# Layer norm moved from GpSimd to VectorE, and one more slot in two weight rings, in a transformer block on eight cores

## The chip, the cores and the metric

The kernel runs on the 8 cores of one Trainium2 chip, one program on every core, with no exchange between them. Cores 0 to 3 work on the first batch element and cores 4 to 7 on the second. The metric is the device time in microseconds of the slowest core.

## The reference

The block adds an attention branch and a feed-forward branch, both fed by the same layer norm, to the input `x` of shape (2, 4096, 2048):

```python
xn = layernorm(x)                                    # over 2048 features
q, k = rope(xn @ Wq.T), rope(xn @ Wk.T)              # 16 heads, each two halves of 64
v = xn @ Wv.T                                        # 16 heads of 128
o1, o2 = softmax(q1 k1 / 8) v, softmax(q2 k2 / 8) v
attn = rmsnorm(o1 - lam * o2) * gamma * (1 - LAMBDA_INIT)
ffn = ((silu(xn @ Wg.T * gs)) * (xn @ Wu.T * us)) @ Wd.T * ds    # 5632 inner features
out = x + attn @ Wo.T + ffn
```

## The kernel before, in words

The program that runs is `build_F` (`build_A` and `build_B` are an older pair that is not launched). A core owns 1024 tokens of the output, but computes K and V for all 4096 tokens of its batch element itself. Activations lie transposed: features on the 128 partitions, tokens along the free dimension, so a tile of x is 128 features by 512 tokens.

**K and V.** The 4096 tokens are taken in four chunks of 1024; chunk 0 holds the core's own tokens. For each chunk come the layer norm (`emit_ln`), the K projection (16 output chunks `och`, each 32 matmuls, L1065, then rope on VectorE and a maximum of squares) and the V projection (`emit_vproj_cache`, eight groups of 64 matmuls, L1455, emptied by ScalarE). In chunk 0 the fp32 weights are cast by their loads and also stored as bf16 copies (`wk_c`, `wv_c`) that the other chunks read.

**Layer norm.** `emit_ln` works on two tiles of 512 tokens. In each it reads x twice, in four quarters of 4 k-chunks (1 MB each), through a ring `rx` of two slots on SyncE's queue (L172):

- The statistics pass: per k-chunk, GpSimd casts x to bf16 (L186), ScalarE squares it (L188), and TensorE sums both over the partitions with a column of ones (L192, L195).
- A short chain on one partition makes mean and 1/sqrt(var + eps) (L200 to L208), and TensorE spreads both over the 128 partitions into PSUM `ps_b` (L212, L214). ScalarE copies them to SBUF as `mB_sb` and `rB_sb` (L217, L218), since GpSimd's operands lie in SBUF.
- The normalise pass: for each of 16 k-chunks GpSimd subtracts the mean (L227) and multiplies by rstd (L229) into the bf16 operand of the projections.

**Feed-forward.** After the Q projection, for each of two tiles of 512 tokens: 44 chunks of gate and up (32 matmuls, L1156 and L1161 in turn, then ScalarE's Silu and two VectorE instructions that end in `h_bf`), and then 16 chunks `hch` of the down projection, each two halves of 22 matmuls (L1200 with the first half of the weights, L1207 with the second). The weights come through rings in one SBUF tensor `wffn`, loaded by GpSimd's DMA queue: `gring` (2 slots, L1147), `uring` (2 slots, L1149) and `dring` (3 slots, L1190 and L1192; a chunk takes two slots).

Then follow attention over all 4096 keys for 16 heads, and the output projection.

**What sets the order.** There is no scheduler. `Prog` keeps one list of instructions for each engine in the order in which the Python code emits them, and each engine runs its list in that order, its waits and the DMAs that it issues included. Each instruction with a count also waits for the one before it on its own engine (except on TensorE). A ring's load waits until the work that `consumed` noted for its slot is done:

```python
        slot = i % n
        if i >= n:
            for sem, val in self.done[i - n].items():
                self.p.wait(self.queue, sem, val)
```

`gring.consumed`, `uring.consumed` and `dring.consumed` note the count of TensorE at the end of the whole chunk, for both of its loads. The first matmul of the K projection waits for the value that `emit_ln` returns (all of the layer norm's arithmetic) and for its `wbuf` load (L1050 in chunk 0, L1057 later), which GpSimd issues.

Of the kernel before, what the change touches and what calls it, by code (L numbers as in the profile page):

```python
# [8 lines left out]
F32 = mybir.dt.float32  # L9
# [116 lines left out]
def alloc_common(nc, ent, t):  # L126
# [18 lines left out]
    t["eps_col"] = ent(nc.sbuf_tensor("eps_col", [128, 1], F32))  # L145
    t["mB_sb"] = ent(nc.sbuf_tensor("mB_sb", [128, 512], F32))
    t["rB_sb"] = ent(nc.sbuf_tensor("rB_sb", [128, 512], F32))
    t["plt"] = ent(nc.sbuf_tensor("plt", [128, 512], F32))
    t["trow"] = ent(nc.sbuf_tensor("trow", [1, 16], F32))
# [14 lines left out]
def emit_ln(p, t, x_hbm, xn_bf, xn_seg, xn_col0, ring=None):  # L164
# [12 lines left out]
    for tile in range(2):  # L177
        p.wait("pe", "dv", t.get("hn_dv", 0))
        for q in range(4):
            i, sl, key = qload(q, tile)  # L180
            p.wait("pool", *key)
            p.wait("act", *key)
            for j in range(4):
                kch = q * 4 + j
                co = sl * 2048 + j * 512
                p.inc("pool", "pl", 1, lambda E, co=co: E.tensor_copy(  # L186
                    xbb[:, co:co + 512], xc[:, co:co + 512]))
                p.inc("act", "ac", 1, lambda E, co=co: E.activation(  # L188
                    x2b[:, co:co + 512], xc[:, co:co + 512], AF.Square))
                p.wait("pe", "pl")  # L190
                p.wait("pe", "ac")
                p.emit("pe", lambda E, co=co, kch=kch: E.matmul(  # L192
                    ps_d1[:], t["ones_col_bf"][:], xbb[:, co:co + 512],
                    start=(kch == 0), stop=(kch == KCH - 1)))
                mmv = p.inc("pe", "pe", 1, lambda E, co=co, kch=kch: E.matmul(  # L195
                    ps_d2[:], t["ones_col_bf"][:], x2b[:, co:co + 512],
                    start=(kch == 0), stop=(kch == KCH - 1)))
            ring.consumed(i, "pl", "ac", "pe")
        p.wait("act", "pe", mmv)
# [10 lines left out]
        p.wait("pe", "dv")  # L210
        p.wait("pe", "pl")
        p.emit("pe", lambda E: E.matmul(ps_b[:, 0:512], t["ones_row_f"][:], row[0:1, 0:512],  # L212
                                        start=True, stop=True))
        bcv = p.inc("pe", "pe", 1, lambda E: E.matmul(  # L214
            ps_b[:, 512:1024], t["ones_row_f"][:], row[0:1, 1536:2048], start=True, stop=True))
        p.wait("act", "pe", bcv)
        p.inc("act", "ac", 1, lambda E: E.activation(t["mB_sb"][:], ps_b[:, 0:512], AF.Copy))  # L217
        brv2 = p.inc("act", "ac", 1, lambda E: E.activation(t["rB_sb"][:], ps_b[:, 512:1024], AF.Copy))  # L218
        for q in range(4):
            i, sl, key = qload(q, tile)  # L220
            p.wait("pool", *key)
            p.wait("pool", "ac", brv2)
            for j in range(4):
                kch = q * 4 + j
                co = sl * 2048 + j * 512
                c0 = xn_col0 + tile * 512
                p.inc("pool", "pl", 1, lambda E, co=co: E.tensor_tensor(  # L227
                    t["plt"][:, 0:512], xc[:, co:co + 512], t["mB_sb"][:], ALU.subtract))
                p.inc("pool", "pl", 1, lambda E, kch=kch, c0=c0: E.tensor_tensor(  # L229
                    xn_bf[:, kch * xn_seg + c0: kch * xn_seg + c0 + 512],  # L230
                    t["plt"][:, 0:512], t["rB_sb"][:], ALU.mult))
            ring.consumed(i, "pl")
    return {"pl": p.ct["pl"]}

# [195 lines left out]
def build_B(debug=False):  # L430
# [30 lines left out]
    t = {}  # L461
# [14 lines left out]
    t["eps_col"] = ent(nc.sbuf_tensor("eps_col", [128, 1], F32))  # L476
    t["mB_sb"] = ent(nc.sbuf_tensor("mB_sb", [128, 512], F32))
    t["rB_sb"] = ent(nc.sbuf_tensor("rB_sb", [128, 512], F32))
    t["plt"] = ent(nc.sbuf_tensor("plt", [128, 512], F32))
    t["bias_sb"] = ent(nc.sbuf_tensor("bias_sb", [128, 16], F32))  # L480
# [414 lines left out]
def build_F(debug=False):  # L895
# [48 lines left out]
    t["eps_col"] = ent(nc.sbuf_tensor("eps_col", [128, 1], F32))  # L944
    t["mB_sb"] = ent(nc.sbuf_tensor("mB_sb", [128, 512], F32))
    t["rB_sb"] = ent(nc.sbuf_tensor("rB_sb", [128, 512], F32))
    t["plt"] = ent(nc.sbuf_tensor("plt", [128, 512], F32))
    t["bias_sb"] = ent(nc.sbuf_tensor("bias_sb", [128, 16], F32))
# [185 lines left out]
    t["h_bf"] = ent2(nc.sbuf_tensor("h_bf", [128, ICH * 512], BF16, side="right"))  # L1134
    t["wffn"] = ent2(nc.sbuf_tensor("wffn", [128, 8448], BF16, side="right"))
    gring = Ring(p, "rg", 2, "pool")
    uring = Ring(p, "ru", 2, "pool")
    dring = Ring(p, "rd", 3, "pool")
    wffn = t["wffn"]
    UOFF = 4096  # L1140
    for tile in range(2):
# [454 lines left out]
```

How the kernel before makes its waits and increments, by code:

```python
    def wait(self, eng, sem, val=None):  # L41
        v = self.ct[sem] if val is None else val
        if v <= 0:
            return
        s = self.sems[sem]
        self.emit(eng, lambda E, s=s, v=v: E.wait_ge(s, v))
# [3 lines left out]
    def inc(self, eng, sem, n, mk):  # L50
        own = self.OWN.get(eng)
        if own is not None and self.ct[own] > 0:
            self.wait(eng, own)
        if n >= 16 and sem == "lds" and self.ct[sem] > 0:
            self.wait(eng, sem)
        s = self.sems[sem]
        self.ct[sem] += n
        v = self.ct[sem]
        self.emit(eng, lambda E, mk=mk, s=s, n=n: mk(E).then_inc(s, n))
        return v
```

## Time and profile before

| What | us |
|---|---|
| Two timed executions | 6734.73 and 6789.26 |
| Their median | 6761.99 |
| The profiled execution, its own time | 6545.5 |
| Its span, slowest core (core 5) | 6544.0 |
| Shortest core's span (core 4) | 6505.0 |
| TensorE busy in the span | 4297.3 |
| ScalarE busy | 1742.8 |
| VectorE busy | 846.9 |
| GpSimd busy | 608.1 |

The span runs from the first to the last instruction of one core. In the trace PE is TensorE, DVE VectorE, ACT ScalarE, POOL GpSimd and SPq or POOLq the DMA queues of SyncE and GpSimd. A row of a group gives its busy time, the mean of one instruction, and the time that its engine stood idle just before it, with what ended that wait. "PEclk" is the granted TensorE clock as a share of 2.4 GHz; 0.5 is the 1.2 GHz level. Matmul lengths overlap: at the full level one starts 0.216 us after the other though each row shows 0.38.

### The profile page before, as it was taken

The numbers are of one execution on the slowest core, as the hardware profiler recorded it, in microseconds if no ns is written. First come the engines' busy times: TensorE is split into PE (matmuls) and PEld (weight loads), VectorE is DVE, ScalarE is ACT, GpSimd is POOL, SyncE is SP. The second block draws the span as 40 slices with busy tenths as digits, with TensorE's granted clock in tenths as the row PEclk, the third lists the DMA queues.
The fourth block names the chain that finished last, engine by engine and source line by source line (L and its number), as shares of the span: only waits on it lengthen the run. The fifth ranks groups of instructions, "written<-read, shape, count | busy, mean of one in ns | idle before, by whom it ended". The sixth has DMA issues, their size and how long they took to land.

```text
span 6544.0 us, 47810 instructions; the slowest of 8 cores (6505.0 to 6544.0 us)
## 1 busy us (share of the span) xinstructions
PE 4297.3 (66%) x16260; PEld 1362.7 (21%) x16260; DVE 846.9 (13%) x1492; ACT 1742.8 (27%) x1879; POOL 608.1 (9%) x786
## 2 busy tenths in 40 slices
PE   2457255725653566557777777777777878787877
PEld 0113012201221122122233332311111111111113
DVE  0230033003201321321100111000000000000002
ACT  1011110111111111100000000046666666666650
POOL 5100600050024000000100000000000000000000
PEclk6679577856786788679988999888888888888889
DMA  3234311321132122135555555511000100000005
GB/s 112 73 85 152 112 39 58 138 83 40 74 124 77 39 82 84 26 58 97 97 96 97 101 98 93 106 39 26 13 13 13 26 13 13 23 17 13 13 10 145
DMA packets 177301, 428.87 MB, mean 66 GB/s; under 512 B 75944, under 2 KB 75944, under 8 KB 170152
## 3 DMA queue, kind: packets, MB, share of 16 engines
q0 software_dynamic: 55872, 272.65, 19.1%
q1 hardware_dynamic: 121192, 153.16, 7.6%
q8 instruction: 136, 2.23, 0.1%
q14 instruction: 101, 0.83, 0.0%
HBM read 539.02 MB, written 58.72 MB: 91 GB/s over the span
## 4 chain that ended last, share of the span: by engine, by line
PE 61%; DVE 11%; ACT 9%; DMA 8%; issue 6%; POOL 5%; DVEq 0%; ACTq 0%; SPq 0%; POOLq 0%
PE ps_a L1065 9%; PE ps_a L1455 7%; PE ps_b L1292 6%; PE ps_a L1156 5%; PE ps_a L1266 5%; PE ps_a L1161 5%; PE ps_d L1302 5%; PE ps_b L1297 4%; PE ps_d L1306 3%; DMA wffn<-dn 3%; PE ps_b L1207 3%; POOL plt L227 2%; PE ps_a L297 2%; POOL xnb L229 2%; DMA xc<-xTb 2%
## 5 line engine op out<-in xcount | busy, mean ns | idle before, releaser
L1286 ACT ACTIVATE e<-ps_a,bias_sb 128x1024 bf16<-128x1024 f32 x1024 | 1140.3, 1114 | 455.5 <-PE ps_a L1271 452.5
L1156 PE MATMUL ps_a<-xn_bf,wffn 128*128 128x512 bf16 x1408 | 572.8, 407 | 277.7 <-DVE h_bf L1182 259.6
L1161 PE MATMUL ps_a<-xn_bf,wffn 128*128 128x512 bf16 x1408 | 571.5, 406 | 0.0
L260 PE MATMUL ps_d<-sq_b,mask_bf 128*1 128x512 bf16 x160 | 93.6, 585 | 707.0 <-ACT sq_b L255 523.0
L1065 PE MATMUL ps_a<-xnb,wbuf 128*128 128x512 bf16 x1536 | 432.9, 452 | 154.3 <-DMA wbuf<-wk_c 154.3
L1266 PE MATMUL ps_a<-q_bf,ktb 64*128 64x512 bf16 x1024 | 416.2, 413 | 111.2 <-DVE xn_bf L1351 98.8
L1292 PE MATMUL ps_b<-e,vtb 128*128 128x512 bf16 x1024 | 405.2, 396 | 56.2 <-ACT e L1286 42.3
L239 ACT ACTIVATE qraw_bf<-ps_a 128x1024 bf16<-128x1024 f32 x80 | 81.9, 1023 | 1286.7 <-PE ps_a L1065 1057.9
L1271 PE MATMUL ps_a<-q_bf,ktb 64*128 64x512 bf16 x1024 | 417.2, 414 | 0.0
L1297 PE MATMUL ps_b<-e,vtb 128*128 128x512 bf16 x1024 | 406.1, 397 | 0.0
L1306 PE MATMUL ps_d<-e,ones_col_bf 128*1 128x512 bf16 x1024 | 402.4, 393 | 0.0
L1455 PE MATMUL ps_a<-wvbuf,xnb 128*128 128x512 bf16 x1536 | 358.5, 397 | 64.8 <-ACT v_stage L1467 64.8
L1302 PE MATMUL ps_d<-e,ones_col_bf 128*1 128x512 bf16 x1024 | 399.7, 390 | 0.0
L1174 ACT ACTIVATE tmp<-ps_a,gs_sb 128x512 f32<-128x512 f32 x88 | 60.5, 687 | 1116.4 <-PE ps_a L1161 1116.4
L192 PE MATMUL ps_d<-xbb,ones_col_bf 128*1 128x512 bf16 x128 | 70.0, 547 | 296.0 <-POOL xbb L186 293.4
L1065 PEld LDWEIGHTS ps_a<-xnb,wbuf 128*128 128x128 bf16 x1536 | 169.7, 113 | 437.3 <-issue 321.4
L1207 PE MATMUL ps_b<-h_bf,wffn 128*128 128x512 bf16 x704 | 201.4, 454 | 84.5 <-DMA wffn<-dn 84.5
L1329 DVE TENSOR_SCALAR r2B<-r2B,lam_vec 128x512 f32<-128x512 f32 x32 | 15.6, 486 | 1846.8 <-ACT r2B L1327 1846.8
L1156 PEld LDWEIGHTS ps_a<-xn_bf,wffn 128*128 128x128 bf16 x1408 | 145.7, 103 | 499.4 <-issue 362.2
L1376 POOL DMA_DIRECT2D wbuf<-wo x16 | 8.4, 528 | 2233.9 <-issue 2099.6
L1467 ACT ACTIVATE v_stage<-ps_a 128x512 bf16<-128x512 f32 x128 | 76.4, 597 | 516.2 <-PE ps_a L1455 507.5
L1266 PEld LDWEIGHTS ps_a<-q_bf,ktb 64*128 64x128 bf16 x1024 | 93.5, 93 | 572.9 <-issue 572.9
(123 smaller groups left out, 4038.3 us busy)
## 6 DMA issues: line engine op xcount, KB each, us to landing
wffn<-gu POOLq DMA_DIRECT2D x176, 512.0 KB, 7.0
xc<-xTb SPq DMA_DIRECT2D x64, 1024.0 KB, 5.3
wvbuf<-wv_c POOLq DMA_DIRECT2D x28, 2048.0 KB, 8.7
wffn<-dn POOLq DMA_DIRECT2D x64, 704.0 KB, 8.4
wbuf<-wk_c POOLq DMA_DIRECT2D x48, 512.0 KB, 3.5
kT_s<-kstage SPq DMA_DIRECT2D x64, 256.0 KB, 2.4
v_s<-v_stage SPq DMA_DIRECT2D x32, 512.0 KB, 5.5
ktb<-kT_s SPq DMA_DIRECT2D x16, 1024.0 KB, 5.1
```

Source lines behind the costliest of these rows:

```text
L1065: mm = lambda E, och=och, kch=kch, half=half, par=par, slot=slot, xn_dst=xn_dst: E.matmul(t["ps_a"][:, par * 1024 + half * 512: par * 1024 ...
L1156: p.emit("pe", lambda E, kch=kch, par=par, tile=tile, gsl=gsl: E.matmul(t["ps_a"][:, par * 1024: par * 1024 + 512], wffn[:, gsl * 2048 + k ...
L1161: mm = lambda E, kch=kch, par=par, tile=tile, usl=usl: E.matmul(t["ps_a"][:, par * 1024 + 512: par * 1024 + 1024], wffn[:, UOFF + usl * 20 ...
L1207: mm = lambda E, ich=ich, par=par, s1=s1: E.matmul(t["ps_b"][:, par * 512:(par + 1) * 512], wffn[:, s1 * 2816 + (ich - 22) * 128: s1 * 281 ...
L1266: p.emit("pe", lambda E, b=b, par=par, koff=koff, qcol=qcol: E.matmul(ps_a[:, par * 1024: par * 1024 + 512], t["ktb"][0:64, koff + b * 128 ...
L1271: return p.inc("pe", "pe", 1, lambda E, b=b, par=par, koff=koff, qcol=qcol: E.matmul(ps_a[:, par * 1024 + 512: par * 1024 + 1024], t["ktb" ...
L1286: ev = p.inc("act", "ac", 1, lambda E, par=par, h=h: E.activation(t["e12"][:, par * 1024:(par + 1) * 1024], ps_a[:, par * 1024:(par + 1) * ...
L1292: p.emit("pe", lambda E, b=b, par=par, koff=koff, first=first, last=last: E.matmul(ps_b[:, 0:512], t["vtb"][:, koff + b * 128: koff + (b + ...
L1297: p.emit("pe", lambda E, b=b, par=par, koff=koff, first=first, last=last: E.matmul(ps_b[:, 512:1024], t["vtb"][:, koff + b * 128: koff + ( ...
L1302: p.emit("pe", lambda E, par=par, first=first, last=last: E.matmul(ps_d1[:], t["ones_col_bf"][:], t["e12"][:, par * 1024: par * 1024 + 512 ...
L1306: mmD = lambda E, par=par, first=first, last=last: E.matmul(ps_d2[:], t["ones_col_bf"][:], t["e12"][:, par * 1024 + 512: par * 1024 + 1024 ...
L1455: mm = lambda E, kch=kch, tc=tc, tok=tok, slot=slot: E.matmul(vps(tc), xn_bf[:, kch * xn_seg + tok: kch * xn_seg + tok + 128], t["wvbuf"][ ...
```

## The change

The layer norm's arithmetic leaves GpSimd. VectorE casts x in the statistics pass, and in the normalise pass it reads mean and rstd straight from `ps_b` in PSUM, with `tmp0` as the intermediate. The copies `mB_sb`, `rB_sb` and the tensors `mB_sb`, `rB_sb` and `plt` go (6 KB a partition). The waits on GpSimd's count `pl` become waits on VectorE's count `dv`, and two waits of TensorE go: one on `dv` at the start of a tile (the values that it covered are waited for again later) and one on `pl` ahead of the broadcast. `wffn` grows from 8448 to 11264 columns, `gring` gets a third slot and `dring` a fourth; `uring` keeps two.

```diff
@@ emit_ln, statistics pass @@
-        p.wait("pe", "dv", t.get("hn_dv", 0))
         for q in range(4):
             i, sl, key = qload(q, tile)
-            p.wait("pool", *key)
+            p.wait("dve", *key)
             p.wait("act", *key)
...
-                p.inc("pool", "pl", 1, lambda E, co=co: E.tensor_copy(
+                p.inc("dve", "dv", 1, lambda E, co=co: E.tensor_copy(
                     xbb[:, co:co + 512], xc[:, co:co + 512]))
...
-                p.wait("pe", "pl")
+                p.wait("pe", "dv")
                 p.wait("pe", "ac")
...
-            ring.consumed(i, "pl", "ac", "pe")
+            ring.consumed(i, "dv", "ac", "pe")
@@ emit_ln, broadcast and normalise pass @@
-        p.wait("pe", "pl")
...
-        p.wait("act", "pe", bcv)
-        p.inc("act", "ac", 1, lambda E: E.activation(t["mB_sb"][:], ps_b[:, 0:512], AF.Copy))
-        brv2 = p.inc("act", "ac", 1, lambda E: E.activation(t["rB_sb"][:], ps_b[:, 512:1024], AF.Copy))
         for q in range(4):
             i, sl, key = qload(q, tile)
-            p.wait("pool", *key)
-            p.wait("pool", "ac", brv2)
+            p.wait("dve", *key)
+            p.wait("dve", "pe", bcv)
...
-                p.inc("pool", "pl", 1, lambda E, co=co: E.tensor_tensor(
-                    t["plt"][:, 0:512], xc[:, co:co + 512], t["mB_sb"][:], ALU.subtract))
-                p.inc("pool", "pl", 1, lambda E, kch=kch, c0=c0: E.tensor_tensor(
+                p.inc("dve", "dv", 1, lambda E, co=co: E.tensor_tensor(
+                    t["tmp0"][:, 0:512], xc[:, co:co + 512], ps_b[:, 0:512], ALU.subtract))
+                p.inc("dve", "dv", 1, lambda E, kch=kch, c0=c0: E.tensor_tensor(
                     xn_bf[:, kch * xn_seg + c0: kch * xn_seg + c0 + 512],
-                    t["plt"][:, 0:512], t["rB_sb"][:], ALU.mult))
-            ring.consumed(i, "pl")
-    return {"pl": p.ct["pl"]}
+                    t["tmp0"][:, 0:512], ps_b[:, 512:1024], ALU.mult))
+            ring.consumed(i, "dv")
+    return {"dv": p.ct["dv"]}
@@ build_F, feed-forward @@
-    t["wffn"] = ent2(nc.sbuf_tensor("wffn", [128, 8448], BF16, side="right"))
-    gring = Ring(p, "rg", 2, "pool")
+    t["wffn"] = ent2(nc.sbuf_tensor("wffn", [128, 11264], BF16, side="right"))
+    gring = Ring(p, "rg", 3, "pool")
     uring = Ring(p, "ru", 2, "pool")
-    dring = Ring(p, "rd", 3, "pool")
+    dring = Ring(p, "rd", 4, "pool")
     wffn = t["wffn"]
-    UOFF = 4096
+    UOFF = 6144
```

Three places of the program show what moves. The first is VectorE's list at the start of chunk 0. Before the change, two one-row subtracts (one for each tile of 512 tokens) stand between the copy of lambda and the rope work of the K projection:

```order
L993 COPY lam_vec<-ps_b 128x1
L204 TENSOR_TENSOR row<-row 1x512 x2
L241 STREAM_SHUFFLE tswp_bf<-qraw_bf 128x1024
L242 TENSOR_TENSOR tmpa_bf<-qraw_bf,ctab 128x1024
L244 TENSOR_TENSOR tswp_bf<-tswp_bf,stab 128x1024
```

With the change (its line numbers are lower) the same place begins so, with 15 more pairs of subtract and multiply behind the last row before the second tile's casts:

```order
L979 COPY lam_vec<-ps_b 128x1
L182 CAST xbb<-xc 128x512 x16
L200 TENSOR_TENSOR row<-row 1x512
L219 TENSOR_TENSOR tmp<-xc,ps_b 128x512
L221 TENSOR_TENSOR xn_bf<-tmp,ps_b 128x512
```

The 16 casts and 32 arithmetic instructions of each tile now stand in VectorE's list ahead of the rope work of the same chunk.

The second place is GpSimd's list from the V projection of chunk 0 to the K projection of chunk 1. Before, the loads of `wv_c` are followed by the casts and the arithmetic of chunk 1's two tiles, and only then come the `wk_c` loads; this is the second tile's start:

```order
L227 TENSOR_TENSOR plt<-xc,mB_sb 128x512
L229 TENSOR_TENSOR xnb<-plt,rB_sb 128x512
L186 CAST xbb<-xc 128x512 x16
L227 TENSOR_TENSOR plt<-xc,mB_sb 128x512
L229 TENSOR_TENSOR xnb<-plt,rB_sb 128x512
```

With the change there is nothing between the two kinds of loads:

```order
L1428 DMA wv_c<-wvbuf 128x8192
L1432 DMA wvbuf<-wv_c 128x8192 x4
L1043 DMA wbuf<-wk_c 128x2048 x16
L1432 DMA wvbuf<-wv_c 128x8192 x8
L1043 DMA wbuf<-wk_c 128x2048 x16
```

The `wk_c` loads have moved up past 96 instructions of the layer norm on that queue.

The third place is GpSimd's list where the down projection starts, with the semaphores that each row waits for (`pe` is TensorE's count, `pl` GpSimd's own). Before:

```order
L1190 DMA wffn<-dn 128x2816 [waits pe,pl]
L1192 DMA wffn<-dn 128x2816 [waits pl]
L1190 DMA wffn<-dn 128x2816 [waits pl]
L1192 DMA wffn<-dn 128x2816 [waits pe,pl]
L1190 DMA wffn<-dn 128x2816 [waits pe,pl]
```

And with the change:

```order
L1176 DMA wffn<-dn 128x2816 [waits pe,pl]
L1178 DMA wffn<-dn 128x2816 [waits pl]
L1176 DMA wffn<-dn 128x2816 [waits pl]
L1178 DMA wffn<-dn 128x2816 [waits pl]
L1176 DMA wffn<-dn 128x2816 [waits pe,pl]
```

The order of the loads is the same; the second half of the second chunk no longer waits for TensorE to finish the first chunk, and so on for each later second half, which waits for the chunk before last in place of the last.

## Rows read from the trace of the kernel before

**Rows 1.** Stages: length, busy time by engine (count), granted clock, DMA share, GB/s.

```profile
650.00:812.00 162.00, 31.85 (x73) 7.52 (x74) 1.36 (x2) 28.83 (x46) 101.44 (x98) 0.57 0.37 122
1128.00:1277.00 149.00, 121.70 (x513) 51.84 (x512) 1.65 (x4) 19.11 (x32) 3.17 (x6) 0.92 0.28 104
3348.00:3582.00 234.00, 179.65 (x704) 73.85 (x704) 13.33 (x18) 0.00 (x0) 18.54 (x36) 0.86 0.55 100
```

**Rows 2.** Page, the chain that ended last: shares of the span by line.

```profile
PE ps_a L1065 9%; PE ps_a L1455 7%; PE ps_b L1292 6%; PE ps_a L1156 5%; PE ps_a L1266 5%; PE ps_a L1161 5%; PE ps_d L1302 5%; PE ps_b L1297 4%; PE ps_d L1306 3%; DMA wffn<-dn 3%; PE ps_b L1207 3%; POOL plt L227 2%; PE ps_a L297 2%; POOL xnb L229 2%; DMA xc<-xTb 2%
```

**Rows 3.** Groups by line: forms, count | busy us, mean ns | idle before.

```profile
L227 POOL TENSOR_TENSOR plt<-xc,mB_sb 128x512 f32<-128x512 f32 x128 | 161.4, 1261 | 109.4 <-ACT rB_sb L218 92.2
L186 POOL CAST xbb<-xc 128x512 bf16<-128x512 f32 x128 | 78.5, 613 | 238.9 <-DMA xc<-xTb 224.6 <-POOL xbb L186 0.4
L188 ACT ACTIVATE x2b<-xc 128x512 bf16<-128x512 f32 x128 | 80.6, 629 | 291.2 <-DMA xc<-xTb 281.6 <-ACT x2b L188 0.4
```

**Rows 4.** Timeline of chunk 1, first tile: start, length us, engine, line.

```profile
684.81 1.91 PE L214 MATMUL ps_b<-row,ones_row_f 1*128 1x512 f32 x2
688.37 1.26 POOL L227 TENSOR_TENSOR plt<-xc,mB_sb 128x512 f32<-128x512 f32 x1 [11.17 <-ACT rB_sb L218]
...
733.30 2.85 POOL L186 CAST xbb<-xc 128x512 bf16<-128x512 f32 x4
```

**Rows 5.** Groups by line on VectorE, attention stage.

```profile
L1331 DVE TENSOR_TENSOR tmp<-ps_b,r1B 128x512 f32<-128x512 f32 x32 | 22.1, 691 | 3.3
L1349 DVE TENSOR_TENSOR tmp<-tmp,rstdB 128x512 f32<-128x512 f32 x32 | 22.1, 692 | 104.3 <-ACT rstdB L1346 104.3
L1329 DVE TENSOR_SCALAR r2B<-r2B,lam_vec 128x512 f32<-128x512 f32 x32 | 15.6, 486 | 1846.8 <-ACT r2B L1327 1846.8
```

**Rows 6.** Timeline of VectorE in one attention tile.

```profile
5002.94 0.69 DVE L1331 TENSOR_TENSOR tmp<-ps_b,r1B 128x512 f32<-128x512 f32 x1
5003.74 0.69 DVE L1333 TENSOR_TENSOR tmp<-ps_b,r2B 128x512 f32<-128x512 f32 x1
```

**Rows 7.** Landing of x loads (L172): whole span, then 690 to 735 us.

```profile
DMA to landing us min/median/max: 5.0/5.3/14.4
...
DMA to landing us min/median/max: 5.1/5.1/5.1
```

**Rows 8.** Timeline of chunk 0, then the chain of chunk 1: into the K projection.

```profile
182.02 1.26 POOL L229 TENSOR_TENSOR xn_bf<-plt,rB_sb 128x512 bf16<-128x512 f32 x1
190.39 1.86 PE L1065 MATMUL ps_a<-xn_bf,wbuf 128*128 128x512 bf16 x4 [53.55 <-DMA wbuf<-wk]
...
806.33 1.27 POOL xnb L229
...
811.94 8.75 PE ps_a L1065 x32
```

**Rows 9.** Down matmuls: two groups by line, then the line L1207 (min/median/max).

```profile
L1207 PE MATMUL ps_b<-h_bf,wffn 128*128 128x512 bf16 x704 | 201.4, 454 | 84.5 <-DMA wffn<-dn 84.5
L1200 PE MATMUL ps_b<-h_bf,wffn 128*128 128x512 bf16 x704 | 160.4, 385 | 16.6 <-DMA wffn<-dn 16.6
...
L1207 PE MATMUL ps_b<-h_bf,wffn x704: 376/379/634, 3361.3 to 4282.5; 128*128 128x512 bf16 x176
```

**Rows 10.** Timeline of the first down stretch.

```profile
3366.78 0.53 POOL L1192 DMA_DIRECT2D wffn<-dn  x1 [17.16 <-PE ps_b L1207]
3374.26 6.59 PE L1207 MATMUL ps_b<-h_bf,wffn 128*128 128x512 bf16 x22 [3.34 <-DMA wffn<-dn]
...
3486.47 4.91 PE L1207 MATMUL ps_b<-h_bf,wffn 128*128 128x512 bf16 x22 [2.13 <-DMA wffn<-dn]
```

**Rows 11.** Landing of the `dn` loads: first halves (L1190), then second halves (L1192).

```profile
DMA to landing us min/median/max: 7.2/9.1/14.0
...
DMA to landing us min/median/max: 5.9/6.3/10.9
```

**Rows 12.** The group of gate matmuls.

```profile
L1156 PE MATMUL ps_a<-xn_bf,wffn 128*128 128x512 bf16 x1408 | 572.8, 407 | 277.7 <-DVE h_bf L1182 259.6 <-DMA wffn<-gu 18.1
```

More of the change, by code:

```diff
@@ L145, in alloc_common @@
     t["eps_col"] = ent(nc.sbuf_tensor("eps_col", [128, 1], F32))
-    t["mB_sb"] = ent(nc.sbuf_tensor("mB_sb", [128, 512], F32))
-    t["rB_sb"] = ent(nc.sbuf_tensor("rB_sb", [128, 512], F32))
-    t["plt"] = ent(nc.sbuf_tensor("plt", [128, 512], F32))
     t["trow"] = ent(nc.sbuf_tensor("trow", [1, 16], F32))
@@ L476, in build_B @@
     t["eps_col"] = ent(nc.sbuf_tensor("eps_col", [128, 1], F32))
-    t["mB_sb"] = ent(nc.sbuf_tensor("mB_sb", [128, 512], F32))
-    t["rB_sb"] = ent(nc.sbuf_tensor("rB_sb", [128, 512], F32))
-    t["plt"] = ent(nc.sbuf_tensor("plt", [128, 512], F32))
     t["bias_sb"] = ent(nc.sbuf_tensor("bias_sb", [128, 16], F32))
@@ L944, in build_F @@
     t["eps_col"] = ent(nc.sbuf_tensor("eps_col", [128, 1], F32))
-    t["mB_sb"] = ent(nc.sbuf_tensor("mB_sb", [128, 512], F32))
-    t["rB_sb"] = ent(nc.sbuf_tensor("rB_sb", [128, 512], F32))
-    t["plt"] = ent(nc.sbuf_tensor("plt", [128, 512], F32))
     t["bias_sb"] = ent(nc.sbuf_tensor("bias_sb", [128, 16], F32))
@@ L1134, in build_F @@
     t["h_bf"] = ent2(nc.sbuf_tensor("h_bf", [128, ICH * 512], BF16, side="right"))
-    t["wffn"] = ent2(nc.sbuf_tensor("wffn", [128, 8448], BF16, side="right"))
-    gring = Ring(p, "rg", 2, "pool")
+    t["wffn"] = ent2(nc.sbuf_tensor("wffn", [128, 11264], BF16, side="right"))
+    gring = Ring(p, "rg", 3, "pool")
     uring = Ring(p, "ru", 2, "pool")
-    dring = Ring(p, "rd", 3, "pool")
+    dring = Ring(p, "rd", 4, "pool")
     wffn = t["wffn"]
-    UOFF = 4096
+    UOFF = 6144
     for tile in range(2):
```

## The prediction

> **What bounds the kernel now.** I read the stage table first [rows 1]. In the layer-norm stretch 650 to 812 us TensorE is busy 32 of 162 us and GpSimd 101; in the down stretch 3348 to 3582 us TensorE is busy 180 of 234 us, at a granted clock of 0.86. The kernel has eight such layer-norm tiles (two per chunk) and two down stretches. The shares of the chain that ended last [rows 2] name what stands there: GpSimd's L227 and L229 and the loads of `dn` and of x are on it, beside the long TensorE stages that the change leaves alone. The table of groups gives the durations [rows 3], and the timeline of one tile the order [rows 4]: the broadcast matmul L214 ends at 686.72, GpSimd's first subtract starts at 688.37, after ScalarE's two copies, and GpSimd works without a gap until 733.30, when it casts the first quarter of the next tile. So the normalise pass is GpSimd's alone, 44.9 us a tile, and the statistics pass is paced by ScalarE, which takes 629 ns beside a cast of 613 ns, and by the loads of x that both wait for.
>
> **The change part by part.**
>
> *Normalise pass.* One k-chunk costs GpSimd a subtract (L227, 1261 ns) and a multiply (L229), with 1.404 us from start to start (32 of them in 44.93 us). VectorE is to do the same two. Its multiply with one fp32 operand in PSUM takes 691 ns, and one with both in SBUF 692 ns [rows 5]; two dependent ones start 0.80 us apart [rows 6]. So 32 x 0.797 = 25.5 us in place of 44.9: 19.4 us a tile, 155.5 us over eight. Both ends for the instruction not seen in this exact pairing: 486 ns (L1329, the quickest VectorE pass over 512 fp32 elements here [rows 5]) gives another 50 us, 1261 ns (GpSimd's own) gives nothing; I take 691, a row of nearly the same form. The Trainium skill (VectorE: DVE Perf Modes, The TRN2 errata) states a fixed cost of 120 cycles for a VectorE operation with a PSUM source against 58 from SBUF. By that table 256 instructions would give back about 17 us, an estimate from its 0.96 GHz. The two rows of 691 and 692 ns show no such difference, and the measurement decides.
>
> *Does the load keep up?* Each quarter of x (1 MB) will be eaten in 6.4 us in place of 11.2. In the normalise pass a quarter landed 5.1 us after its issue [rows 7], and with two slots it has the 6.4 us of its neighbour: 1.3 us to spare. That cover is thin, and a rival below rests on it. The next tile's first quarters keep their distance to the end of this pass, so its statistics pass is as long as before.
>
> *ScalarE's two copies* go. GpSimd started 1.65 us after the matmul's end; VectorE needs about 0.15 for the hop: 1.5 us a tile, 12 us. *The casts* move to VectorE. Its one-input pass takes 486 ns and its slowest row of this size 692; by the first the cast lies within ScalarE's 629 ns, by the second 0.06 us x 128 = 8 us stick out. It has one input in SBUF like L1329, so I take 486 and a cost of nothing; if ScalarE were quicker, the cast would set the pace with 0.6 us. In VectorE's queue the casts stand behind the previous chunk's K work, finished a whole V stretch (149 us) before, and the tile-end subtract L204 stands behind normalise work that it waited for anyway through the statistics.
>
> *GpSimd's queue is empty of arithmetic.* So the first two `wbuf` loads of a chunk, which stood behind 96 GpSimd instructions of the layer norm, are issued in the V stretch before, where they have the whole layer-norm stretch of 162 us to land. The last GpSimd instruction ended at 183.28 and the K projection started at 190.39; in chunk 1 it was 807.60 and 811.94 [rows 8]. That is 7.1 and 4.3 us, and I take 4.3 for the other two: 20 us, less 0.3 us each for the semaphore: 19 us. Bounds 0 (something else is late too) and 20.
>
> *Down projection.* TensorE waited 84.5 us for the second half of `dn` (L1207), 30 times, and two starts of a stage for the first half (L1200) [rows 9]. With three slots the second half of chunk h+1 may be issued only when chunk h has ended; in the timeline it is issued at 3366.78 and TensorE waits until 3374.26 [rows 10]. With four it is issued a whole chunk earlier. The 84.5 us go, the two starts stay. What is late next? A chunk's matmuls at the 2.4 GHz level are 44 x 4.75 / 22 = 9.5 us (L1207 started at 3486.47 and lasted 4.91 with the last drain, about 4.75 to the next start). The transfers of a chunk, both issued 0.55 us apart, land after 6.3 and 9.1 us at the median [rows 11], so a pair needs 9.65 us and has until the chunk after next. The two are nearly level.
>
> *The clock in the down stage.* After the wait the 22 matmuls took 6.59 us, and elsewhere 4.91 [rows 10]. L1207 has a mean of 454 ns against a median of 379 and a maximum of 634 [rows 9]: (454 - 379) / (634 - 379) = 29% of 704, or 207 matmuls, ran at the 1.2 GHz level; L1200, mean 385, adds 17. At half rate each starts 0.21 us later: 224 x 0.21 = 47 us. The Trainium skill (TensorE: Matmul & The Clock Gate, Part 1) says that the throttled state is the default and activity lifts it. By that rule all 47 come back; by the row alone none need, since some gaps of 2 us, as before 3486.47, cost no clock at all. The V stretch, almost without gaps, shows 0.92 [rows 1]. I take 40, bounds 0 and 47. Down: 84.5 + 40 = 125 us, bounds 60 (transfers stretched, below) and 131.
>
> *The gate ring's third slot.* TensorE waits there for VectorE's `h_bf`, 259.6 us of L1156's idle time, and for a load only 18.1 us at two starts [rows 12]. The `gate` load is issued one chunk earlier, the `up` load not, and TensorE needs both: nothing. On GpSimd's queue the `up` load now goes ahead of the next `gate` load when a chunk ends, where it stood behind one, so it isn't slowed. Bounds: 18 us lost (the starts take twice as long) and 18 won.
>
> *Sum.* 155.5 + 12 + 19 + 125 = 311 us. The profiled execution took 6545.5 us (span 6544.0, so 1.5 us lie around it) and would take 6234. The two runs shown, 6734.7 and 6789.3, are 3% longer than it, with a median of 6762; I take the same 311 us off that: **6451 us**, 4.6% less.
>
> **The rivals.**
>
> *B, transfers bound the down stage.* A chunk reads 2 x 128 x 2816 x 4 bytes = 2.88 MB. To do that every 9.5 us in place of 14 ((234 - 10) / 16 [rows 1]), all eight cores draw half as much again. For it: L1190's slowest landing is 14.0 us [rows 11]. Against it: the DMA engines are busy 0.55 of that stretch [rows 1], and 0.55 x 14 = 7.7 us of their time fit into 9.5. If a pair takes 12.5 us, the gain is 32 x (14.0 - 12.5) = 48, and with little of the clock back some 60 in all: 6451 + 65 = 6516.
>
> *C, the x loads bound the normalise pass.* It begins once a quarter lands later than 6.4 us. For it: the slowest of the 64 x loads took 14.4 us. Against it: the median of all is 5.3, and all four in one normalise pass took 5.1 [rows 7]. At 8 us a quarter the pass takes 32 us: 8 x 6.5 = 52 us less gain, 6503.
>
> *D, slower: VectorE's PSUM operand.* Place: the 256 instructions that read the broadcast mean and rstd from `ps_b` while x comes from SBUF as fp32. If each took 2.6 us start to start, a tile would take 83 us, 38 more than now: 8 x 38 = 306 us lost against 156 from the other terms: 6762 + 306 - 156 = 6912. It decides from 2.0 us on, where a tile loses the 19.5 us that the others bring. Against it: 691 ns [rows 5].
>
> *E, the fourth slot does nothing*, because issue order on GpSimd or the landing itself holds the halves: the 125 us fall away, 6762 - 186 = 6576.
>
> *F, within 2%:* C and E together leave 311 - 52 - 125 = 134 us, 6628.
>
> **How the numbers follow.** Forecast 0.61, B 0.18, C 0.09, E 0.05, F 0.05, D 0.02. A measurement of this kernel can tell about 2% from no change, 135 us. Forecast, B, C and E lie beyond it: faster 0.93; F gives same 0.05; D slower 0.02. The forecast's own spread is 280 to 330 us. To that comes the spread of the executions of before, 6545.5 to 6789.3: taken from the shortest, the best case is 6545 - 325 = 6220; the upper end takes in B: 6530.
>
> **What would show it.** Right: VectorE's subtract and multiply at 0.69 us, 25 to 26 us a tile; the K projection's first matmul under 0.5 us after the last of them; no wait for `dn` at the second half but at most the first chunk, and a mean near 390 ns for those matmuls; a layer-norm stretch of about 116 us in place of 162; gate and up, K, V and attention stretches as before. Wrong: waits of VectorE for `xc` within the normalise pass (C); waits for `dn` at every chunk (B); a VectorE mean above 0.8 us (D); a lower granted clock in the stages the change leaves alone, which no term here contains.

## Result and profile after

The changed kernel took 6484.3 us (median of 12 executions, 6223.8 to 6646.1), the kernel before 6721.9 us (median of 10, 6558.5 to 6867.0). The ratio is 0.9488 with a 95% interval of 0.9448 to 0.9529. The prediction was 6451 us in a range of 6220 to 6530.

Executions of one kernel differ by up to 7%, and in the long ones the four cores of one die, or of both, show a lower granted clock; what follows therefore compares dies (by the median span of their four cores) that lie within 0.5% of the shortest of their kernel. Their median is 6527 us for the kernel before (32 dies) and 6217 us for the changed one (18 dies): 310 us or 4.7% less, where 311 us were forecast. The ratio above, from the slowest core of each execution, says 5.1%. In the profiled execution the slowest core is core 3 with 6261.2 us; its granted clock is 0.816, and that of core 5, which is read below because the rows of before are core 5's too, is 0.820 at a span of 6224.3 us.

The stage table of the changed kernel, core 5 (stretch, length, busy time by engine with count, granted clock, DMA share, GB/s), answers to [rows 1]. The stretches are one chunk's layer norm, its V projection, a first gate and up stretch and a down stretch:

```profile
601.00:720.00 119.00, 33.60 (x74) 8.53 (x75) 59.00 (x98) 26.45 (x42) 0.00 (x0) 0.56 0.48 151
1037.00:1178.00 141.00, 113.54 (x513) 49.99 (x512) 1.66 (x4) 19.11 (x32) 4.22 (x8) 0.98 0.32 118
2675.00:3162.00 487.00, 343.12 (x1410) 142.43 (x1411) 63.48 (x88) 31.53 (x45) 47.79 (x91) 0.91 0.55 97
3162.00:3322.00 160.00, 154.79 (x704) 69.09 (x702) 12.01 (x16) 0.00 (x0) 17.43 (x33) 0.98 0.80 140
```

Chunk 1's layer norm takes 118.7 us from the issue of its first load of x to the first K matmul (600.86 to 719.52) where it took 159.3 (652.66 to 811.94). The first down stretch takes 156.2 us from its first matmul to the end of its last (3161.60 to 3317.82) where it took 223.2 (3354.83 to 3578.01), at a granted clock of 0.98 in place of 0.86 and with the DMA engines busy 0.80 of the time in place of 0.55. GpSimd is idle in the layer norm and VectorE busy for 59 us. Over the whole core the time went like this:

| Part (core 5) | before us | after us | difference | forecast |
|---|---|---|---|---|
| four layer norms, first load of x to first K matmul | 652.9 | 470.2 | -182.7 | -186.5 |
| feed-forward, first load to the first attention matmul | 1432.7 | 1297.4 | -135.3 | -125 |
| all else | 4458.4 | 4456.7 | -1.7 | 0 |
| span | 6544.0 | 6224.3 | -319.7 | -311 |

The groups by line of the layer norm, core 5 (form, count | busy us, mean ns | idle just before and its releasers), answer to [rows 3]:

```profile
L219 DVE TENSOR_TENSOR tmp<-xc,ps_b 128x512 f32<-128x512 f32 x128 | 88.0, 687 | 60.5 <-PE ps_b L209 46.1 <-DMA xc<-xTb 1.3 <-DVE xn_bf L221 0.5
L221 DVE TENSOR_TENSOR xnb<-tmp,ps_b 128x512 bf16<-128x512 f32 x96 | 66.0, 687 | 10.0
L182 DVE CAST xbb<-xc 128x512 bf16<-128x512 f32 x128 | 54.6, 427 | 547.0 <-DMA xc<-xTb 535.9 <-DVE xbb L182 1.0
L184 ACT ACTIVATE x2b<-xc 128x512 bf16<-128x512 f32 x128 | 80.6, 630 | 236.8 <-DMA xc<-xTb 227.4
```

Subtract and multiply cost 687 ns, with 0.80 us from one to the next in the rows below (139.79, 140.59). The cast costs 427 ns, well inside ScalarE's 630. In the normalise pass VectorE waited for x for 1.3 us in all ("DMA xc<-xTb 1.3"), so the loads kept up with the faster pass. The timeline of core 5 at the end of chunk 0's and of chunk 1's layer norm answers to [rows 8]:

```profile
139.79 0.69 DVE L219 TENSOR_TENSOR tmp<-xc,ps_b 128x512 f32<-128x512 f32 x1
140.59 0.69 DVE L221 TENSOR_TENSOR xn_bf<-tmp,ps_b 128x512 bf16<-128x512 f32 x1
141.53 1.87 PE L1051 MATMUL ps_a<-xn_bf,wbuf 128*128 128x512 bf16 x4 [26.03 <-DVE xn_bf L221]
...
718.59 0.69 DVE L221 TENSOR_TENSOR xnb<-tmp,ps_b 128x512 bf16<-128x512 f32 x1
719.52 2.72 PE L1051 MATMUL ps_a<-xnb,wbuf 128*128 128x512 bf16 x6 [26.42 <-DVE xnb L221]
```

The K projection starts 0.25 us after the last multiply ends (140.59 + 0.69 = 141.28 to 141.53; 719.28 to 719.52), where it had started 7.1 and 4.3 us after it.

The groups of the down and gate matmuls, core 5, answer to [rows 9] and [rows 12]:

```profile
L1193 PE MATMUL ps_b<-h_bf,wffn 128*128 128x512 bf16 x704 | 157.2, 379 | 0.0
L1186 PE MATMUL ps_b<-h_bf,wffn 128*128 128x512 bf16 x704 | 162.5, 388 | 15.8 <-DMA wffn<-dn 15.8
L1142 PE MATMUL ps_a<-xn_bf,wffn 128*128 128x512 bf16 x1408 | 571.0, 406 | 277.1 <-DVE h_bf L1168 258.7 <-DMA wffn<-gu 18.4
```

The landing of the `dn` loads of the same core, in the views of the lines that issue them, first halves (L1176) and second halves (L1178), answers to [rows 11]:

```profile
DMA to landing us min/median/max: 6.1/7.5/13.5
...
DMA to landing us min/median/max: 8.1/10.4/18.1
```

The 704 matmuls of the second half now have a mean of 379 ns, the length at the 2.4 GHz level, and no wait for `dn` is left there; 15.8 us of such waits remain at the first half, 13.8 of them at the two starts of a stretch. First halves now land sooner than before (7.5 us at the median, 9.1 before), second halves later (10.4 us, 6.3 before; the slowest 18.1), and yet TensorE hardly waits. The timeline shows how close the two are:

```profile
3192.77 4.91 PE L1186 MATMUL ps_b<-h_bf,wffn 128*128 128x512 bf16 x22
3197.52 4.91 PE L1193 MATMUL ps_b<-h_bf,wffn 128*128 128x512 bf16 x22
3203.01 4.91 PE L1186 MATMUL ps_b<-h_bf,wffn 128*128 128x512 bf16 x22 [0.57 <-DMA wffn<-dn]
3207.75 4.91 PE L1193 MATMUL ps_b<-h_bf,wffn 128*128 128x512 bf16 x22
```

From 3192.77 to 3197.52 are 4.75 us, the forecast time of a half chunk. At 3203.01 TensorE had waited 0.57 us for a first half: the transfers are just behind it there.

### The profile page after: what moved, and what is told of

Its sections match the earlier page's. It is cut to its first block, busy times and chain, and to the rows that moved or that the text cites. A ratio compares the mean times of both kernels' runs of the same rounds, so it can differ in the third digit from the quotient of the medians.

```text
span 6261.2 us, 47774 instructions; the slowest of 8 cores (6203.0 to 6261.2 us)
## 1 busy us (share of the span) xinstructions
PE 4259.8 (68%) x16260; PEld 1357.8 (22%) x16260; DVE 1077.4 (17%) x1876; ACT 1734.2 (28%) x1863; POOL 206.7 (3%) x402
## 4 chain that ended last, share of the span: by engine, by line
PE 63%; DVE 14%; ACT 10%; DMA 6%; issue 5%; DVEq 1%; ACTq 0%; SPq 0%; POOLq 0%; POOL 0%
PE ps_a L1051 9%; PE ps_a L1441 7%; PE ps_b L1278 6%; PE ps_a L1142 6%; PE ps_a L1147 5%; PE ps_a L1252 5%; PE ps_d L1288 5%; PE ps_b L1283 4%; PE ps_d L1292 4%; PE ps_a L289 2%; DMA xc<-xTb 2%; PE ps_b L1186 2%; PE ps_b L1193 2%; ACT e L1272 2%; DVE tswp_bf L233 2%
## 5 line engine op out<-in xcount | busy, mean ns | idle before, releaser
L1051 PE MATMUL ps_a<-xnb,wbuf 128*128 128x512 bf16 x1536 | 447.4, 464 | 77.4 <-DVE xnb L221 77.4
L1315 DVE TENSOR_SCALAR r2B<-r2B,lam_vec 128x512 f32<-128x512 f32 x32 | 15.6, 486 | 1850.7 <-ACT r2B L1313 1850.7
L1441 PEld LDWEIGHTS ps_a<-wvbuf,xnb 128*128 128x128 bf16 x1536 | 154.7, 102 | 274.9 <-issue 123.6
L1165 DVE TENSOR_SCALAR tmp<-ps_a,us_sb 128x512 f32<-128x512 f32 x88 | 66.0, 750 | 832.1 <-ACT tmp L1160 832.1
## 6 DMA issues: line engine op xcount, KB each, us to landing
wvbuf<-wv_c POOLq DMA_DIRECT2D x28, 2048.0 KB, 10.3
```

The costliest lines, as they stand in the source:

```text
L1051: mm = lambda E, och=och, kch=kch, half=half, par=par, slot=slot, xn_dst=xn_dst: E.matmul(t["ps_a"][:, par * 1024 + half * 512: par * 1024 ...
L1441: mm = lambda E, kch=kch, tc=tc, tok=tok, slot=slot: E.matmul(vps(tc), xn_bf[:, kch * xn_seg + tok: kch * xn_seg + tok + 128], t["wvbuf"][ ...
```

## Experiments

All spans given are medians over dies, formed as in the section above, against 6527 us for before and 6217 us for the changed kernel; the dies of one kernel lie within 20 us of their median, most within 10. The ratio to before is given with its 95% interval where the record has one.

**Only the layer norm (ln_only).** The changed kernel with the rings of before:

```diff
-    t["wffn"] = ent2(nc.sbuf_tensor("wffn", [128, 11264], BF16, side="right"))
-    gring = Ring(p, "rg", 3, "pool")
-    dring = Ring(p, "rd", 4, "pool")
-    UOFF = 6144
+    t["wffn"] = ent2(nc.sbuf_tensor("wffn", [128, 8448], BF16, side="right"))
+    gring = Ring(p, "rg", 2, "pool")
+    dring = Ring(p, "rd", 3, "pool")
+    UOFF = 4096
```

Expected:

> The layer norm on VectorE, with the rings of before (gate 2, down 3 slots). My theory: the gain of 311 us is the sum of two independent parts, and this one brings its 186 us (ratio about 0.971): layer-norm stretches of 113 to 119 us in place of 159 to 162, first matmul of the K projection under 0.5 us after VectorE's last multiply; the waits for the second half of dn stay at 80 to 90 us with a mean near 454 ns for those matmuls. Rival: part of the gain needs the rings too (the transfers of one stage press on the other), then the ratio is above 0.975 or the dn waits differ.

Measured: 6347 us, 180 less than before; ratio 0.9746 (0.9642 to 0.985), an interval too wide to tell the forecast 0.971 from the rival's 0.975. The down matmuls of core 7, groups by line:

```profile
L1193 PE MATMUL ps_b<-h_bf,wffn 128*128 128x512 bf16 x704 | 199.2, 451 | 85.4 <-DMA wffn<-dn 85.4
L1186 PE MATMUL ps_b<-h_bf,wffn 128*128 128x512 bf16 x704 | 162.4, 388 | 14.1 <-DMA wffn<-dn 14.1
```

The waits for `dn` (85.4 us) and the mean of 451 ns are those of before, so the rival that let them differ falls. The layer norm's part stands alone, with 6 us less than forecast.

**Only the rings (rings_only and rings_only2).** The kernel before with the new rings. Its three helper tensors are allocated with the K and V stage's tensors, where alone they are used, so that the larger `wffn` has room. That tells something of the change: `wffn` grows by 5,632 bytes a partition, and the 6 KB of the helper tensors, which the layer norm's part of the change gives back, make up for it.

```diff
-    t["mB_sb"] = ent(nc.sbuf_tensor("mB_sb", [128, 512], F32))
...
+    t["mB_sb"] = entk(nc.sbuf_tensor("mB_sb", [128, 512], F32, side="right"))
...
-    t["wffn"] = ent2(nc.sbuf_tensor("wffn", [128, 8448], BF16, side="right"))
-    gring = Ring(p, "rg", 2, "pool")
+    t["wffn"] = ent2(nc.sbuf_tensor("wffn", [128, 11264], BF16, side="right"))
+    gring = Ring(p, "rg", 3, "pool")
...
-    dring = Ring(p, "rd", 3, "pool")
+    dring = Ring(p, "rd", 4, "pool")
...
-    UOFF = 4096
+    UOFF = 6144
```

(`rB_sb` and `plt` move in the same way as `mB_sb`.)

Expected, of the first and of the second run:

> The new rings (gate 3, down 4 slots) with the layer norm still on GpSimd; the three helper tensors are only live in the K/V stage so that wffn fits. My theory: 125 us less than before (ratio about 0.981), layer-norm stretches of 159 to 162 us as before, no dn wait beyond about 18 us, mean 379 to 390 ns for both halves of the down matmuls. Rival B (transfers bound): waits for dn of over 30 us, about 60 us gained (ratio 0.991).

> The same kernel as rings_only, since its executions were all disturbed. Theory: 125 us less than before, cores at 6390 to 6425 us, ratio about 0.981; together with the 186 us of the layer norm alone (its cores at 6337 to 6364) that makes the whole change, so the parts add. Rival: they do not add (fewer than 100 or more than 150 us here).

Measured: 6398 us in the first run (three dies) and 6400 in the second, 127 less than before. The groups of the second run, core 5:

```profile
L1207 PE MATMUL ps_b<-h_bf,wffn 128*128 128x512 bf16 x704 | 157.2, 379 | 0.0
L1200 PE MATMUL ps_b<-h_bf,wffn 128*128 128x512 bf16 x704 | 161.8, 387 | 20.3 <-DMA wffn<-dn 20.1
L1156 PE MATMUL ps_a<-xn_bf,wffn 128*128 128x512 bf16 x1408 | 570.9, 405 | 277.7 <-DVE h_bf L1182 259.8 <-DMA wffn<-gu 18.0
```

No wait for `dn` at L1207, and 379 ns. With 180 + 127 = 307 us the two parts give the whole change (310): they add, within the spread. Rival B falls: the transfers of a down chunk fit into TensorE's 9.5 us.

**The gate ring back to two slots (gate2).** One number changed in the changed kernel (`Ring(p, "rg", 2, "pool")`). Expected:

> The changed kernel with the gate ring back at two slots. My theory: the third gate slot brings nothing, since TensorE waits there for VectorE: the same time as the changed kernel within 0.3% (ratio to before 0.949), gate and up stretch unchanged (TensorE's idle time for h_bf 259 us, for gu 15 to 21 us). Rival: the slot relieves the load queue, and the time is over 20 us longer.

Measured: 6217.5 us against the changed kernel's 6217; the ratio, 0.9578 (0.9333 to 0.9823), has an interval too wide to tell by itself. The group of gate matmuls, core 5:

```profile
L1142 PE MATMUL ps_a<-xn_bf,wffn 128*128 128x512 bf16 x1408 | 567.6, 403 | 277.7 <-DVE h_bf L1168 258.8 <-DMA wffn<-gu 18.9
```

The waits are the same as with three slots. The third gate slot brings nothing in this kernel.

**The K weights late again (late_w).** After `emit_ln`, one wait in front of GpSimd's loads:

```diff
         psfree = emit_ln(p, t, xTb[:, c0:c0 + 1024], xn_dst, 1024, 0, ring=lnring)
+        p.wait("pool", "dv")
```

Expected:

> The changed kernel with one more wait: GpSimd issues the wbuf loads of a chunk only when VectorE has done that chunk's layer norm. My theory: this gives back the hand-off term, 19 us in all (K projections start 7 us after the last multiply in chunk 0 and 4.3 to 5.3 in the others), ratio about 0.952. Rival: the loads were not what was late, and nothing changes.

Measured: 6230 us, 12.5 more than the changed kernel; ratio 0.9547 (0.9506 to 0.9588). The timeline of core 3 at chunk 1:

```profile
758.95 0.69 DVE L221 TENSOR_TENSOR xnb<-tmp,ps_b 128x512 bf16<-128x512 f32 x1
760.35 1.14 POOL L1044 DMA_DIRECT2D wbuf<-wk_c  x2 [166.50 <-DVE xnb L221]
764.02 1.44 PE L1052 MATMUL ps_a<-xnb,wbuf 128*128 128x512 bf16 x3 [30.15 <-DMA wbuf<-wk_c]
```

The K projection again starts 4.4 us after the last multiply (759.64 to 764.02), and late in the other chunks too (6.2, 4.3 and 4.5 us). By these rows the wait costs 19.4 - 4 x 0.25 = 18.4 us; the span shows 12.5. The sign and the place are shown; the 6 us between the two figures lie within the spread of the dies.

**Mean and rstd read from SBUF (sbuf_stats).** ScalarE's two copies put back, VectorE reads them:

```diff
+        p.wait("act", "pe", bcv)
+        p.inc("act", "ac", 1, lambda E: E.activation(t["mB_sb"][:], ps_b[:, 0:512], AF.Copy))
+        brv2 = p.inc("act", "ac", 1, lambda E: E.activation(t["rB_sb"][:], ps_b[:, 512:1024], AF.Copy))
...
-            p.wait("dve", "pe", bcv)
+            p.wait("dve", "ac", brv2)
...
-                    t["tmp0"][:, 0:512], xc[:, co:co + 512], ps_b[:, 0:512], ALU.subtract))
+                    t["tmp0"][:, 0:512], xc[:, co:co + 512], t["mB_sb"][:], ALU.subtract))
...
-                    t["tmp0"][:, 0:512], ps_b[:, 512:1024], ALU.mult))
+                    t["tmp0"][:, 0:512], t["rB_sb"][:], ALU.mult))
```

Expected:

> The changed kernel with ScalarE's two copies put back, so that VectorE reads mean and rstd from SBUF. My theory: VectorE's subtract and multiply keep 0.69 us (a PSUM operand costs nothing here), and the copies with their semaphores stand in front of each tile: 1.4 us x 8 = 11 to 12 us more than the changed kernel (cores at 6215 to 6240). Rival: the PSUM operand costs 65 ns an instruction, so this gives 17 us back and takes 12: 5 us less than the changed kernel.

Measured: 6235 us, 17 more than the changed kernel; ratio 0.9589 (0.9519 to 0.9659). The groups by line, core 2:

```profile
L222 DVE TENSOR_TENSOR tmp<-xc,mB_sb 128x512 f32<-128x512 f32 x128 | 88.6, 692 | 72.7 <-ACT rB_sb L213 57.3 <-DMA xc<-xTb 2.5 <-DVE xnb L224 0.5
L224 DVE TENSOR_TENSOR xnb<-tmp,rB_sb 128x512 bf16<-128x512 f32 x96 | 66.4, 692 | 10.0
```

With both operands in SBUF an instruction takes 692 ns, with one in PSUM 687. So the PSUM operand is not dearer but 5 ns cheaper: 256 x 5 ns = 1.3 us. The Trainium skill's larger fixed cost for PSUM sources (VectorE: DVE Perf Modes, The TRN2 errata) is not seen in an instruction whose other operand lies in SBUF. VectorE now waits 57.3 us for ScalarE's copies where it waited 46.1 for the broadcast matmul, 11.2 us for eight tiles. That and 1.3 make 12.5 of the 17 us. The four layer norms of core 5 took 15.6 us more than in the changed kernel (485.8 and 470.2), so nearly all of the loss lies there.

**A gap put back by hand (gap).** In the changed kernel each down chunk's second half waits for four short ScalarE copies that start when the first half is done (the part left out lets the last matmul of the first half count up TensorE's semaphore):

```diff
...
             p.wait("pe", *k1)
+            p.wait("act", "pe")
+            for _g in range(4):
+                gapv = p.inc("act", "ac", 1, lambda E: E.activation(
+                    t["tmp1"][:, 512:1024], t["tmp1"][:, 512:1024], AF.Copy))
+            p.wait("pe", "ac", gapv)
```

Expected:

> The changed kernel with an idle gap put back between the two halves of each down chunk: ScalarE runs four copies of 0.6 us each (2.8 to 3.1 us with the semaphores) which TensorE waits for; no load is late. My theory: the gap of before cost TensorE more than its own length, since the matmuls behind it ran partly at the 1.2 GHz level. So 32 gaps of about 3 us cost 96 us of waiting and another 35 to 50 us of slower matmuls: 130 to 145 us more than the changed kernel, mean of the second half's matmuls near 450 ns. Rival: the lower clock of before had another cause (the loads, power), then 96 us and a mean near 380 ns.

Measured: 6385 us, 167 more than the changed kernel; ratio 0.9762 (0.9725 to 0.9799). The down matmuls of core 5 by line (L1202 is the second half):

```profile
L1202 PE MATMUL ps_b<-h_bf,wffn 128*128 128x512 bf16 x704 | 221.3, 488 | 99.6 <-ACT tmp L1198 99.6
L1186 PE MATMUL ps_b<-h_bf,wffn 128*128 128x512 bf16 x704 | 162.0, 387 | 14.1 <-DMA wffn<-dn 14.1
```

One chunk and the second half of the next in the timeline of the same core:

```profile
3207.19 2.80 ACT L1198 ACTIVATE tmp<-tmp 128x512 f32<-128x512 f32 x4 [11.64 <-PE ps_b L1186]
3210.13 6.42 PE L1202 MATMUL ps_b<-h_bf,wffn 128*128 128x512 bf16 x22 [3.10 <-ACT tmp L1198]
3216.39 4.91 PE L1186 MATMUL ps_b<-h_bf,wffn 128*128 128x512 bf16 x22
3224.40 7.81 PE L1202 MATMUL ps_b<-h_bf,wffn 128*128 128x512 bf16 x22 [3.09 <-ACT tmp L1198]
```

All waits of the second half end with ScalarE and none with a load, and still the 22 matmuls behind the gap take 6.42 and 7.81 us and those of the next first half 4.91. By the working of the prediction, (488 - 379) / 255 = 43% of 704 or 301 matmuls ran at the 1.2 GHz level, at 0.21 us each 63 us; with the waits of 99.6 us that makes 163. Each gap also costs the 0.16 us by which a matmul's row otherwise overlaps the next start (4.91 - 4.75), 5 us in 32 gaps, and the 167 are accounted for. So these gaps cost 1.7 times their length (167 / 99.6), and in the kernel before the waits for loads cost 1.6 times theirs by the same working ((84.5 + 0.21 x 207 + 30 x 0.16) / 84.5). The rival that looked for the lower clock elsewhere falls: here a gap without a late load brings it back, and in the changed kernel the granted clock rose to 0.98 while the DMA share rose too, from 0.55 to 0.80.

It was more than I expected (35 to 50 us of slower matmuls). Thirty of the 32 gaps here are 3.1 us long and two 3.4, and behind each of them 6.5 to 13.6 matmuls ran at the lower level, by the same working. Those of before vary: on core 5, of the 14 waits at L1207 that were shorter than 2.4 us, five left the clock as it was and behind each of the nine others about 8 matmuls ran at the lower level, and of the 16 longer ones only one, of 3.79 us, cost nothing. One of each kind, from the timeline of the kernel before:

```profile
3402.36 6.59 PE L1207 MATMUL ps_b<-h_bf,wffn 128*128 128x512 bf16 x22 [2.21 <-DMA wffn<-dn]
...
4264.59 4.91 PE L1207 MATMUL ps_b<-h_bf,wffn 128*128 128x512 bf16 x22 [3.79 <-DMA wffn<-dn]
```

**TensorE freed from the last h_bf (gu_free and gu_free2).** The waits for `h_bf`, 258.7 us, are the largest that is left in the feed-forward part. `ps_a` has a half for even and one for odd chunks, but TensorE waited for the chunk just before, which uses the other half:

```diff
         gufree = {"dv": p.ct["dv"]}
+        gfree = [dict(gufree), dict(gufree)]
...
-            for sem, val in gufree.items():
+            for sem, val in gfree[par].items():
                 p.wait("pe", sem, val)
...
             gufree = {"dv": p.ct["dv"]}
+            gfree[par] = dict(gufree)
```

Expected, of the first and of the second run:

> The changed kernel, and in the gate and up stage TensorE waits for the h_bf of the chunk before last (whose half of ps_a it overwrites), not of the last. Theory: the h_bf waits were what bounded that stage and made the third gate slot worthless; without them a chunk costs TensorE 32 x 0.216 = 6.9 us, and the loads of 2.1 MB (8.1 to 8.7 us per chunk in this stage) bound it: 88 x (10.9 - 8.5) = about 210 us less than the changed kernel, with waits for gu in nearly every chunk. Rival: the loads pack closer and TensorE bounds at about 7.1 us a chunk: 330 us less, hardly any wait for gu.

> The same kernel as gu_free, whose profile was disturbed on one die. Theory: the undisturbed die of that run gives the time, 5887 to 5920 us, ratio about 0.905; TensorE's waits for gu are about 25 us in all and the gate and up chunks take 7.1 us at the 2.4 GHz level.

Measured: 5899 us in the first run and 5902 in the second, 315 less than the changed kernel; ratio to before 0.9031 (0.8996 to 0.9066) in the second. The groups of gate and up matmuls of core 0 in the second run:

```profile
L1143 PE MATMUL ps_a<-xn_bf,wffn 128*128 128x512 bf16 x1408 | 536.4, 381 | 25.4 <-DMA wffn<-gu 24.5
L1148 PE MATMUL ps_a<-xn_bf,wffn 128*128 128x512 bf16 x1408 | 536.3, 381 | 0.0
```

The stage table of core 5 in the same run for 320 us of a gate and up stretch (columns as in the first table of this part):

```profile
2680.00:3000.00 320.00, 308.21 (x1404) 135.62 (x1405) 62.08 (x86) 30.82 (x44) 43.81 (x83) 0.99 0.83 144
```

My theory was that the loads would bound the stage at 8.5 us a chunk; the rival was right. TensorE is at the 2.4 GHz level throughout (0.99), waits 24.5 us for `gu`, and a chunk of 32 matmuls takes 7.3 us (320 / (1404 / 32)). The error was to take the time that a pair of loads needs from issue to landing for the time in which it occupies the queue: the DMA share rises from 0.55 to 0.83, and at the median a `gate` load lands after 8.2 us (7.2 in the changed kernel) and an `up` load after 6.3 (5.2), yet a pair comes every 7.3 us.

**The same with two gate slots (gu_free_g2).** Expected:

> As gu_free, with the gate ring at two slots. Theory: now the third gate slot matters: with two slots both loads of a chunk start only when its slot's chunk has ended and have one chunk's time (7 us) against a landing of 7 to 8 us, so this is 50 to 100 us slower than gu_free, with waits for gu at every chunk. Rival: the up ring has two slots in either kernel and bounds both alike: the same within 15 us.

Measured: 6010 us, 108 more than gu_free and slightly above the 50 to 100 expected; ratio to before 0.9214 (0.9176 to 0.9251). The gate matmuls of core 2:

```profile
L1143 PE MATMUL ps_a<-xn_bf,wffn 128*128 128x512 bf16 x1352 | 518.6, 384 | 115.4 <-DMA wffn<-gu 115.2
L1148 PE MATMUL ps_a<-xn_bf,wffn 128*128 128x512 bf16 x1408 | 539.9, 383 | 7.5 <-DMA wffn<-gu 4.3 <-issue 0.5
```

TensorE waits 115.2 us for `gu` where it waited 24.5. The up ring has two slots in both kernels, so that isn't what bounds; the slot that was worth nothing is worth 108 us as soon as the wait that hid its absence is gone.

## Why the prediction was right

- **The bounds now.** Right: the layer norm and the feed-forward part gave all of the gain but 1.7 us on core 5. That small rest is a sum of two signs: the four V stretches are 13.6 us shorter (563.4 to 549.8 in all) and the four K stretches 7.7 us longer (1223.4 to 1231.1), which no term contained. One trace of each kernel can't tell whether the change did it: in the kernel before the V sum alone runs from 544.9 to 563.4 us over the eight cores.
- **Normalise pass, 155.5 us.** Right. The instruction took 687 ns against the 691 taken, 0.79 us from start to start, and the eight passes of core 5 took 203.7 us in place of 358.4, 154.7 less.
- **The loads keep up (rival C).** Right, with little to spare as said: 1.3 us of waits for x in all 32 quarters of core 5, 3.0 on core 3. C didn't happen, though 8 of those quarters landed later than its 6.4 us, the slowest after 8.8: six of the eight were among the first two of a pass, which are issued before it begins. The statistics passes, however, did not stay as long as before: they took 264.1 us in all in place of 259.2, 4.9 us that the sum put at nothing.
- **ScalarE's copies, 12 us, and the PSUM operand.** Right in size: from the broadcast matmul to the first subtract were 13.4 us in eight tiles and are 1.4 (0.17 each, where 0.15 was taken), and sbuf_stats gave 11.2 back. D, the only way to a slower kernel, asked for 2 us an instruction from start to start and met 0.79.
- **Casts hidden.** Right, 427 ns beside 630.
- **Hand-off, 19 us.** Right: 21.8 us in four chunks of core 5 became 1.0; by the rows of late_w it is 18.4 us, by its span 12.5. For the two chunks not read the prediction took 4.3 us, and they had 5.1 and 5.3. The layer norm as a whole gave 154.7 + 12.0 + 20.8 - 4.9 = 182.6 us on core 5, and 180 in ln_only, against 186.5 forecast.
- **Down projection, 84.5 + 40 us.** Right. From the first `dn` matmul to the next stage's first matmul the first stretch took 231.7 us (3354.83 to 3586.50) and takes 165.1 (3161.60 to 3326.66), the second took 230.3 (4065.01 to 4295.32) and takes 168.2 (3803.44 to 3971.62): 66.6 and 62.1 us less, 128.7 in all, under the upper bound of 131; the rings alone measured 127. The waits inside the two stretches fell by 82.5 us (84.5 are gone at the second half, 2.0 are new at the first), and the 30 waits had also cost 0.16 us of overlap each, 5 us that the sum left out. Of the 47 us of the clock some 42 came back: all of the 43.5 at the second half, as L1193's 379 ns shows, while at the first half 25 matmuls run at the lower level where 17 did ((388 - 379) / 255 x 704), behind the two starts. So 40 was near and a choice between bounds, not a derivation. By the rule of the Trainium skill that I had weighed (TensorE: Matmul & The Clock Gate, Part 1) all 47 would have come back, and the trace agrees in the main: the lower level is left only behind the two starts, after waits of 6.9 us each. The row that spoke for none, a 2 us gap that cost no clock, was one of five such among 14.
- **B and E.** Both fell: no `dn` wait at the second half, 15.8 us at the first, 13.8 of them at the two starts. The other 6.6 us of the feed-forward part lie in the gate and up stretches (3.8 us shorter) and in the two starts of a down stretch (2.7 us), and no term contained them.
- **Gate slot, nothing.** Right (gate2), and for the reason given (gu_free_g2).
- **The time itself.** The sum, 311 us, was right to 1 us by the medians of the dies and 9 us short on core 5. That it came so close is luck in part: on core 5 the layer norm gave 3.8 us less than its term and the feed-forward part 10.3 us more. That 6451 came within 33 us of 6484 is luck too. The two executions shown had a median of 6762 and the ten that were run 6722; from that the same sum gives 6411, 73 us too low. The medians of all executions fell by 238 us only; the executions spread from 6558 to 6867 us before and from 6224 to 6646 us after, which the sum doesn't contain.

## What to carry over

Price a wait of TensorE at its length and at the matmuls behind it: here gaps of 2 to 4 us cost 1.6 to 1.7 times their length, because 29% and 43% of the matmuls behind them ran at the lower level. Before a ring gets another slot, look which wait ends last at the consumer: the same slot was worth 0 behind a wait for VectorE and 108 us without it, while the down ring, of which a chunk takes two slots, needed its fourth. And an engine that both computes and issues loads, like GpSimd here, delays the loads of the next stage; moving its arithmetic away pays twice (154.7 us by the faster instructions, some 20 by the earlier loads).

## What was not expected

- Landing time is not occupancy. The `gate` and `up` loads, 2.1 MB a chunk, landed 8.2 and 6.3 us after their issue, and TensorE could still be fed every 7.3 us with a third slot; the DMA share then was 0.83.
- An idle gap of 3.1 us, put in every time, cost 5.2 us (167 / 32).
- A VectorE instruction with one fp32 operand in PSUM took 687 ns, 5 ns less than with both in SBUF.
